# Attention maxima written into the query rows by GpSimd instead of by transfers, and scores issued ahead of the maxima blocks

## The reference

```python
scores = jnp.einsum('bqhd,bkhd->bhqk', q, k) / jnp.sqrt(jnp.float32(Dh))   # 16 heads, Dh = 8, 2048 tokens
attn = jax.nn.softmax(scores, axis=-1)                                     # stages F and H: no mask
ctx = jnp.einsum('bhqk,bkhd->bqhd', attn, v)                               # stage L: the same, causal mask
```

## Time and profile before

| what | value |
|---|---|
| median of 3 runs | 3215.1 us (3196.74, 3215.1, 3217.59) |
| the profiled execution | 3210.34 us, its span 3208.5 us |
| mean granted TensorE clock | 0.883 of full |
| busy share PE / DVE / ACT / POOL | 87% / 66% / 53% / 7% |
| stage F, first maxima block to last score item | 502.8 to 1260.9 us |

### The profile page before, as it was taken

One profiled execution on the slowest core, in us unless ns is written; L12 is line 12 of the kernel. 1 busy time (PEld: TensorE's weight loads), 2 busy tenths in 40 slices (PEclk: granted clock), 3 DMA queues, 4 the chain that ended last, 5 costly groups with the idle time before them and its releaser, 6 DMA issues. The chain is left out here.

```text
span 3208.5 us, 62945 instructions
## 1 busy us (share of the span) xinstructions
PE 2795.7 (87%) x20985; PEld 1217.1 (38%) x20985; DVE 2123.1 (66%) x4016; ACT 1714.2 (53%) x2055; POOL 214.6 (7%) x469
## 2 busy tenths in 40 slices
PE   6788857999999997999599999939998989896998
PEld 2688842222222232444244444422222223222443
DVE  5544467988888894322578777648988979784222
ACT  4222223776677676433166656624776767675343
POOL 1222210000000000000100000010000000000000
PEclk8888856998898898899699999967989989888999
DMA  1000001110110110211111111110111011010211
GB/s 43 1 0 0 0 17 65 36 33 22 36 35 23 34 36 22 78 41 39 69 40 47 53 38 53 48 65 30 32 36 33 24 35 35 20 36 22 79 59 33
DMA packets 89023, 115.82 MB, mean 36 GB/s; under 512 B 19645, under 2 KB 62615, under 8 KB 86383
## 3 DMA queue, kind: packets, MB, share of 16 engines
q1 hardware_dynamic: 85561, 110.38, 11.2%
q10 hardware_dynamic: 3248, 2.21, 0.3%
HBM read 78.39 MB, written 20.55 MB: 31 GB/s over the span
## 5 line engine op out<-in xcount | busy, mean ns | idle before, releaser
L536 DVE TENSOR_REDUCE Hmaxes<-Hm 128x1 f32<-128x512 f32 x1024 | 626.8, 682 | 108.5 <-PE Hm L440 108.4
L536 DVE TENSOR_REDUCE Fmaxes<-Fm 128x1 f32<-128x512 f32 x1024 | 626.5, 682 | 99.3 <-PE Fm L440 99.3
L497 ACT ACTIVATE Hprob<-Hs 128x1024 f32<-128x1024 f32 x512 | 522.4, 1025 | 208.2 <-PE Hs L401 165.2
L497 ACT ACTIVATE Fprob<-Fs 128x1024 f32<-128x1024 f32 x512 | 522.4, 1025 | 200.7 <-PE Fs L401 158.4
L536 DVE TENSOR_REDUCE Lmaxes<-Lm 128x1 f32<-128x512 f32 (+3 forms) x640 | 354.2, 605 | 111.9 <-PE Lm L440 54.5
L497 ACT ACTIVATE Lprob<-Ls 128x1024 f32<-128x1024 f32 (+7 forms) x384 | 294.1, 777 | 182.3 <-PE Ls L401 99.0
L419 PE MATMUL Fo<-Fprob,Fvh 128*32 128x256 f32 x4096 | 339.9, 419 | 0.3 <-ACT Fprob L497 0.3
L419 PE MATMUL Ho<-Hprob,Hvh 128*32 128x256 f32 x4096 | 337.8, 416 | 0.3 <-ACT Hprob L497 0.3
L440 PE MATMUL Hm<-Hka,Hqa 48*128 48x512 bf16 x1024 | 291.7, 419 | 42.7 <-DVE Hmaxes L536 16.5
L440 PE MATMUL Fm<-Fka,Fqa 48*128 48x512 bf16 x1024 | 294.1, 422 | 38.3 <-DVE Fmaxes L536 15.4
L401 PE MATMUL Hs<-Hqa,Hka 51*128 51x512 bf16 x1024 | 246.6, 407 | 34.6 <-DMA Hqa<-Htoprow 27.6
(11 more groups left out here) (426 smaller groups left out, 3072.2 us busy)
## 6 DMA issues: line engine op xcount, KB each, us to landing
FEwb<-FE_weights SPq DMA_DIRECT2D x8, 1024.0 KB, 5.5
HEwb<-HE_weights SPq DMA_DIRECT2D x8, 1024.0 KB, 5.5
Fvh<-Fvstack SPq DMA_DIRECT2D x17, 256.0 KB
Lvh<-Lvstack SPq DMA_DIRECT2D x17, 256.0 KB
Hvh<-Hvstack SPq DMA_DIRECT2D x17, 256.0 KB
FEw<-in_L_ffn_W SPq DMA_DIRECT2D x16, 256.0 KB, 2.9
HEw<-in_L_ffn_W SPq DMA_DIRECT2D x16, 256.0 KB, 2.9
Fqa<-F_qparts SPq DMA_DIRECT2D x34, 96.0 KB
```

Source lines behind the costliest of these rows:

```text
L497: nc.scalar.activation(prob[:, :, :].rearrange("p k q -> p (k q)")[:, lo:hi], sps[n % 2][:, o:o + hi - lo], ACT.Exp, scale=SCALE).then_inc ...
L536: nc.vector.reduce_max(maxes[:, a, t, half:half + 1], src[:, 0:w], AX.X).then_inc(max_free, 1)
```

## The change

GpSimd gets more work. After its four splitting instructions it waits for the turned rows and then writes them into `qa` itself: each of two instructions multiplies 12 rows of `toprow` (3 parts by 4 query tiles) by a mask `pick` that keeps each row only in the 128 columns of its own tile, so 12 rows with 512 columns are written, once for each group. These rows now stand at partitions 0 to 11 and 64 to 75, below the 48 main rows, and the maxima blocks read all 60 rows too; for them the 12 rows have to be zero. So GpSimd also clears these rows of the slot for head h+2 (function `clear`, two instructions with 2048 columns), after `maxima(h, 1)` and before `maxima(h+1, 0)`, and TensorE waits for `cleared` ahead of the first maxima block of a head. The six transfers of `tops` leave the SyncE queue. In the first block the one memset of `ka` becomes four memsets of 32 rows of `ka` and `qa`, the memset of `vstack` waits for them, and so do the first query loads. TensorE issues `score` k ahead of `share[k]`. MARGIN becomes 5200 for F and H and 4100 for L; by the planner's arithmetic this makes LEAD 47 in F and H (turns are now the first piece of `share[11]` and of `share[27]`; three blocks go with item 16 still) and leaves L's plan as it is.

```diff
-SROWS = MAIN + PARTS
+TROWS = 4 * PARTS
+ROWS = TROWS + MAIN
...
-                nc.gpsimd.memset(ka[:, :, :], -1.0).then_inc(filled, 1)
+                for r in range(GROUPS):
+                    nc.gpsimd.memset(ka[64 * r:64 * r + 32, :, :], -1.0).then_inc(filled, 1)
+                    nc.gpsimd.memset(qa[64 * r:64 * r + 32, :, :], 0.0).then_inc(filled, 1)
+                pool.wait_ge(filled, 4)
                 nc.gpsimd.memset(vstack[:, :, :, :], 1.0).then_inc(ones, 1)
...
                 sp.wait_ge(q_stored, 32)
+                sp.wait_ge(filled, 4)
                 load_q(sp, 0, 0)
...
-    MARGIN = 3600
+    MARGIN = 4100 if causal else 5200
...
-                def tops(h, a, s, c):
-
-                    sp.wait_ge(max_free, c)
-                    for r in range(GROUPS):
-                        cols = slice(a * HALF + r * BANK, a * HALF + (r + 1) * BANK)
-                        for part in range(PARTS):
-                            row = 64 * r + MAIN + part
-                            sp.dma_start(qa[row:row + 1, s, cols].rearrange("o (t q) -> o t q", t=4),
-                                         toprow[part * 8 + 4 * r:part * 8 + 4 * r + 4, :]).then_inc(top_in, 16)
...
                     if n == 0:
-                        pe.wait_ge(top_in, (2 * h + a + 1) * TOPS)
+                        pe.wait_ge(top_in, (2 * h + a + 1) * GROUPS)
...
                     for k in range(NS):
+                        a, n = (0, k) if k < NSCORE[0] else (1, k - NSCORE[0])
+                        score(h, u, a, n)
                         for a, j, ahead in share[k]:
                             if last and ahead:
                                 continue
                             if ahead and (a, j) == (0, 0):
 
                                 pe.wait_ge(loaded[(u + 1) % SLOTS], (i + (u + 1) // SLOTS + 1) * LOADS)
+                                pe.wait_ge(cleared, 2 * (h + 1))
                             item(h + ahead, (u + ahead) % SLOTS, a, j, mps[slot(h + ahead, a, j)], count(h + ahead, a, j))
-                        a, n = (0, k) if k < NSCORE[0] else (1, k - NSCORE[0])
-                        score(h, u, a, n)
...
+                    nc.gpsimd.tensor_tensor(low, halves(top[:, 1, :]), middle, ALU.subtract).then_inc(top_split, 1)
+
+                    pool.wait_ge(max_free, c)
+                    for r in range(GROUPS):
+                        rows = slice(64 * r, 64 * r + TROWS)
+                        cols = slice(a * HALF + r * BANK, a * HALF + (r + 1) * BANK)
+                        nc.gpsimd.tensor_tensor(qa[rows, s, cols].rearrange("k (t q) -> k t q", t=4),
+                                                toprow[rows, :].unsqueeze(1).broadcast_to([TROWS, 4, P]),
+                                                pick4(r), ALU.mult).then_inc(top_in, 1)
+                    pool.wait_ge(top_in, GROUPS * (u + 1))
+
+                def clear(h, s):
+
+                    pool.wait_ge(weighed, RING + NK * h)
+                    for r in range(GROUPS):
+                        rows = slice(64 * r, 64 * r + TROWS)
+                        nc.gpsimd.tensor_tensor(qa[rows, s, :], ka[rows, s, :], ka[rows, s, :], ALU.subtract)\
+                            .then_inc(cleared, 1)
+                    pool.wait_ge(cleared, 4 + GROUPS * h)
+
+                def head(h, u, first=False, last=False):
+                    maxima(h, 1, u % SLOTS, count(h, 1, "turn"))
+                    if not first and not last:
+                        clear(h, (u + 2) % SLOTS)
+                    if not last:
+                        maxima(h + 1, 0, (u + 1) % SLOTS, count(h + 1, 0, "turn"))
```

More of the change, by code:

```diff
@@ L102, in attention @@
     ka = heads.enter_context(nc.sbuf_tensor(name + "ka", [P, SLOTS, T], BF16))
-    topp = heads.enter_context(nc.sbuf_tensor(name + "topp", [P, P // 8, 8], BF16))
+    topp = heads.enter_context(nc.sbuf_tensor(name + "topp", [P, GROUPS, P // 8, 4], BF16))
     nothing = heads.enter_context(nc.sbuf_tensor(name + "nothing", [P, 8], F32))
@@ L112, in attention @@
     kept = semaphore(nc, heads, name + "kept")
+    cleared = semaphore(nc, heads, name + "cleared")
     loaded = [semaphore(nc, heads, f"{name}loaded{s}") for s in range(SLOTS)]
     LOADS = 16 * (2 * GROUPS * PARTS + 1)
-    FIRST_ROW = [sum(PARTS - b for b in range(a)) * DH for a in range(PARTS)]
+    FIRST_ROW = [TROWS + sum(PARTS - b for b in range(a)) * DH for a in range(PARTS)]
     def load_q(sp, h, s):
@@ L343, in _ @@
                     load_kv(sp, h, h)
-                tops(0, 0, 0, count(0, 0, "turn"))
                 def head(h, u, first=False, last=False):
[L347 to L350, removed]
+                    if causal and not first:
+                        spread(h - 1)
                     if not last:
@@ L397, in score @@
                         r = q0 // BANK
-                        rows = slice(64 * r, 64 * r + SROWS)
+                        rows = slice(64 * r, 64 * r + ROWS)
                         diag = causal and q0 == kt * P - a * HALF
@@ L430, in item @@
                         pe.wait_ge(top_split, 2 * h + a + 1)
[L431 removed]
+                        nc.tensor.transpose(out[:, 0:P // 2].bitcast(BF16), topp[:, :, :, :].rearrange("p r a t -> p (r a t)"),
                                             ident_bf[:, :]).then_inc(max_in, 1)
@@ L436, in item @@
                     r = kb % GROUPS
-                    rows = slice(64 * r, 64 * r + MAIN)
+                    rows = slice(64 * r, 64 * r + ROWS)
                     lo = kb * BANK
@@ L510, in _, with maxima @@
             def _(pool):
-                def split_maxima(h, a):
+                pick4 = lambda r: pick[64 * r:64 * r + TROWS, :].unsqueeze(2).broadcast_to([TROWS, 4, P])
+                def maxima(h, a, s, c):
                     u = 2 * h + a
+                    halves = lambda x: x.rearrange("p (r t) -> p r t", r=GROUPS)
+                    high, middle, low = (topp[:, :, part, :] for part in range(PARTS))
                     pool.wait_ge(topped, u + 1)
-                    nc.gpsimd.tensor_tensor(topp[:, 0, :], top[:, 0, :], nothing[:, :], ALU.add).then_inc(chain, 1)
+                    nc.gpsimd.tensor_tensor(high, halves(top[:, 0, :]), halves(nothing[:, :]), ALU.add).then_inc(chain, 1)
@@ L515, in split_maxima @@
                     pool.wait_ge(chain, u * 3 + 1)
-                    nc.gpsimd.tensor_tensor(top[:, 1, :], top[:, 0, :], topp[:, 0, :], ALU.subtract).then_inc(chain, 1)
+                    nc.gpsimd.tensor_tensor(halves(top[:, 1, :]), halves(top[:, 0, :]), high, ALU.subtract)\
+                        .then_inc(chain, 1)
                     pool.wait_ge(chain, u * 3 + 2)
-                    nc.gpsimd.tensor_tensor(topp[:, 1, :], top[:, 1, :], nothing[:, :], ALU.add).then_inc(chain, 1)
+                    nc.gpsimd.tensor_tensor(middle, halves(top[:, 1, :]), halves(nothing[:, :]), ALU.add).then_inc(chain, 1)
@@ L527, in _ @@
+                maxima(0, 0, 0, count(0, 0, "turn"))
+                for u in range(SLOTS):
+                    head(u, u, first=(u == 0))
+                with pool.Fori(1, (NH - 1) // SLOTS) as i:
+                    for u in range(SLOTS):
+                        head(i * SLOTS + u, u)
+                head(NH - 1, 0, last=True)
             @block.vector
@@ L1457, in constant_table @@
         "mask2_qk": folded(np.where(r > c, BIG, 0.0)),
+        "pick": np.where(r % 64 < TROWS, r % 4 == np.arange(4)[None, :], 0.0),
         "iota": np.broadcast_to(np.arange(E_N)[None, :], (P, E_N)),
```

24 lines of the change are left out of this document (9 added, 15 removed).

## The result

The changed kernel takes 3329.58 us (median, 3321.49 to 3331.7), the kernel before 3212.99 us in the same comparison: a ratio of 1.037, with a 95% interval of 1.033 to 1.041. Forecast were 3130 us. The profiled execution has a span of 3319.7 us, 111.2 us more than before, and a mean clock of 0.872.

The account below looks back on a forecast made before the run. VectorE was taken to bound the steady state, with late transfers and lower clocks lengthening divide windows. 3210.3 - 66.4 (transfers) - 18.6 (order, lead) = 3125.3 us, with the runs' median 4.8 us above: 3130 us, range 3095 to 3240.

Parts of the forecast that it names:

- 66.4 us for the transfers: Second-half-turn windows of F and H return to 21.92 us without the late transfers: 32.7 us in F, 33.7 in H.
- 18.6 us for order and lead: Scores ahead of blocks and larger LEAD shorten VectorE's idle gaps: 0.3 us in each of 62 F and H windows.
- third rival: Masked writes are slow, over 2.3 us each, so items 16 and 0 wait: 186 us, 3316 us; chance 0.04.
- start within 0.1 us of each other: Sign of being right: GpSimd's two masked writes, on different partitions, start almost together.
- 21.6 to 22 us forecast: Sign of being right: windows with a divide take this long at clock 1.00, except those with a loop jump.
- second rival: The clock fall belongs to the stretch, not the wait: only 32 of 66.4 us return, 3164 us; chance 0.10.
- a sign of being wrong: Among the listed signs against the forecast: clocks below 1 in windows with no wait.
- 0.33 us gap: VectorE's idle time at item 16 in a clean window, where the score waits for its transfers; it can go.
- gap behind the turn: VectorE's 0.22 us idle time after the turn in a clean window; it can go.
- In F and H these are 16 items apart, about 20 us, and the cost is 0.: GpSimd's clears and TensorE's need of the next split, queued behind them, lie that far apart: no cost.
- overlap of instructions on different partitions: Two GpSimd instructions on disjoint partitions run together, so clears in L and the first block's fills cost 0.
- first rival: GpSimd works instructions one by one: 84 us in L, 22.4 us for first blocks, 3236 us; chance 0.20.

Follow-up runs that it names:

- e6: e1 with the first block's four fills made two of 128 partitions, the first query load waiting for that of qa alone; 3133.99 us, ratio 0.975.
- e7: e6 with TensorE's old order, the blocks of an item ahead of its scores; 3130.75 us, ratio 0.974.
- e10: e7 with the margin back at 3600, so LEAD is 44 again in F and H; 3123.37 us, ratio 0.973.
- e8: The kernel before with TensorE's new order alone, transfers and margin as they were; 3342.8 us, ratio 1.040.
- e5: e1 with a spare 12 x 4096 fill ahead of the clearing fills, GpSimd busy as long as in the changed kernel; 3201.37 us, ratio 0.997.
- e2: The changed kernel with the divide eight items later in F and H (item 24), where no clear runs; 3195.65 us, ratio 0.994.
- e9: The kernel before with two extra 12 x 2048 GpSimd instructions reading spare tiles behind second-half turns of heads 1 to 14; 3272.43 us, ratio 1.020.
- e3: The changed kernel with a head's clears moved behind the writes of the next head's first half; 3192.31 us, ratio 0.993.
- e1: The changed kernel with the clears made as fills that only write, a 12 x 8 addition ahead carrying the wait; 3155.25 us, ratio 0.982.

## Why the prediction was wrong

*The gain was nearly right, as a whole.* The forecast summed 66.4 us for the transfers and 18.6 us for order and lead, 85 us. With the three costs out, e6 is 79 us under the kernel before, and at 3134 us where 3130 were forecast. By the windows of the two traces, the 30 windows of F and H with a second-half turn gave 55 us and the 24 without one and without a loop jump gave 8 us. The masked writes take 2.14 us for both, inside the 1.4 to 2.7 us given, and no score waits for them: the third rival is out. The two don't start within 0.1 us of each other, as they were to; they take 1.03 us each, one after the other.

*The clock follows the wait, but a smaller wait than was thought.* With the transfers gone, most windows with a divide in e6 are at 1.00 and 22.1 us, just above the 21.6 to 22 us forecast. So the fall did not belong to the stretch alone, and the second rival, by which half of each loss would have stayed, is out as it was put. But 7 of 28 windows still fall, behind no wait but the 0.62 us of the ordinary divide. The prediction listed a clock below 1 without a wait as a sign of being wrong, and this comes close to it. These windows are part of why 55 us came and not 66.

*The credit for the rest was wrong.* The 18.6 us were put down to scores ahead of the blocks and the larger lead. Windows without a divide did shrink, by 0.24 to 0.4 us. But e7 and e10 have the gain without the new order and without the new lead, and the new order itself costs 0.1 us a window. What shortened them is that the first score of a half no longer waits, which the prediction had named as the 0.33 us gap (in these windows it is item 0 of the next head, not item 16). The gap behind the turn, which was to go as well, grew from 0.22 to 0.41 us. Windows with a divide didn't shrink, 22.1 us against 21.92. And taken alone, with the transfers in place, the new order costs 4.0%, 130 us (e8). The prediction said that if a score waits, the blocks of its item wait behind it, and put no price on it.

*The step that failed: "In F and H these are 16 items apart, about 20 us, and the cost is 0."* The clears were costed by who waits for their results. In F and H nobody stands for them. They still hold VectorE's product, so that it takes 2.4 to 3.0 us, TensorE then has no PSUM tile for 3.1 us, and the clock falls. From the changed kernel to e5 this is 128 us, more than the whole loss of 117; moving the divide away gives 134 (e2). e9 shows it added to the kernel before, e3 carried to L. The Trainium skill (SBUF — State Buffer, Who interferes with whom) says that a VectorE instruction with two SBUF inputs contends with a GpSimd instruction that reads SBUF and not with one that only writes. The runs agree with both halves: 2.78 and 2.43 us beside reads, 0.29 us in a fill. The row of the divide's product, 0.29 us once in a head, was too small to be looked at; the forecast should have put the other engine's 3.6 us against it.

*The second failed step: overlap of instructions on different partitions.* 0.06 us of early start was taken as a sign of full overlap. The fills at partitions 0 and 64 run one after the other, the clears too. The prediction had taken overlap from the rule of separate cores in the Trainium skill (GPSIMD Engine Reference, section 2.1, Instruction dispatch), too; here the measurement decides against it, for instructions of 12 and of 32 partitions. Why they don't overlap stays open. The first rival had the mechanism and most of its size: TensorE's wait in L forecast at 2.7 us, measured 2.73. Its price was forecast at 84 us for L and 22 us for the first blocks. Measured are 46 us (e5 to e1) and 21 us (e1 to e6). In L the wait lengthens the short window by 3.2 us at a clock of 1.00, and the long window behind it by 0.7 us on average (19.2 to 21.3 us against 19.9): the clock comes down less than was assumed, and only in part of the heads. By itself this rival would have given 3236 us, 94 us short of the measured time: what it lacked is the first failed step.

The three costs were taken out one after the other (128, 46 and 21 us), so that they sum to the way from 3329.6 to 3134 us holds by construction. What supports the largest of them is that other runs find it again: 134 us when the divide is moved away (e2), and 61 us when the reads alone are put into windows of the kernel before, most of which were long already (e9). The 46 us for L have their like in the table: L takes 44 us more in the changed kernel than in the kernel before, and 31 us more in e3, where its loss is another.

## What to carry to other kernels

Cost an instruction that is moved to another engine by what it holds while it runs, not only by who waits for it: list the other engine's instructions with two SBUF operands that can fall beside it, and take the full length of the moved one as the price, with what a lower clock adds behind it. Clear a tile with a fill, not by subtracting it from itself: it was half as long here and held nobody. In an in-order stream, what stands ahead of a wait is cover for it; move it behind only when the wait is gone.

## What the hardware showed that was not expected

- VectorE's 128 x 128 product of two SBUF operands, 0.29 us alone, takes 2.4 to 3.0 us beside a GpSimd instruction that reads 12 partitions of SBUF. It ends 0.15 us after the instruction that is running (603.34 after 603.19, 1729.13 after 1728.98), and does not wait for the next (e3, e9). The reciprocal with one operand isn't held.
- GpSimd's time goes by columns and not by partitions: 5.21 us for a fill of 32 x 6144 as for 128 x 6144, 3.59 us for 12 x 2048 bf16 as 3.60 us for 128 x 2048 fp32. Two instructions on disjoint partitions take twice the time of one.
- A wait of 3.1 us on TensorE costs 3.1 to 5.6 us in its window, as the clock comes back sooner or later (0.93 against 0.81 in windows that are otherwise alike). After a wait of 0.62 us the clock held in 21 of 28 windows of e6 and fell in 7, at 0.6 to 2.1 us each.
